# Both query, key and value projections of a four-layer network rebuilt as double-buffered stages, the rotary one in two chunks of eight dimensions

## What is computed

```python
# layer 2
q, k, v = split(layernorm(t) @ W_qkv)            # 16 query heads, 4 key/value heads, 16 wide
# layer 3
g_slc, g_swa = sigmoid(h @ Wg_slc.T), sigmoid(h @ Wg_swa.T)
q, k, v = h @ Wq.T, h @ Wk.T, h @ Wv.T
q = q * cos + rotate_half(q) * sin               # rotate_half([x1, x2]) = [-x2, x1], halves of 8
k = k * cos + rotate_half(k) * sin
out = (softmax(causal(q @ k.T / 4)) @ v) * (g_slc + g_swa)
```

## Time and profile before

| | us |
|---|---|
| median of 3 runs | 2603.23 (2596.47 to 2609.32) |
| the profiled execution, its own time | 2597.99 |
| its span | 2596.3 |
| PE busy / weight loads busy | 2256.7 / 1554.8 |
| DVE / ACT / POOL busy | 1496.3 / 1084.5 / 739.0 |
| layer 2's projection: first matmul to attention's first load | 324.81 to 401.09 |
| layer 3's projection: first matmul to attention's first load | 1387.49 to 1537.88 |

### The profile page before, as it was taken

The page is one execution under the profiler, slowest core; times in us unless marked ns, Lnnn a source line. Parts: engine busy times, 40 slices in busy tenths (PEclk is TensorE's granted clock), DMA queues, the critical chain, the costliest instruction groups (busy, mean ns, idle before and its releaser), DMA issues. The chain is left out here.

```text
span 2596.3 us, 45765 instructions
## 1 busy us (share of the span) xinstructions
PE 2256.7 (87%) x13908; PEld 1554.8 (60%) x13909; DVE 1496.3 (58%) x3329; ACT 1084.5 (42%) x2167; POOL 739.0 (28%) x852
## 2 busy tenths in 40 slices
PE   6979576999977999599957859999865999999997
PEld 5757433444455889599953324444443666666675
DVE  3868747888745766366654658888457222232222
ACT  3434453666634443355532316666530222222222
POOL 1424001222200000388842522222100333333332
PEclk9989797999987999799987869999987999999999
DMA  3000033221102000765651221222046322222211
GB/s 114 1 1 0 7 96 84 54 52 50 39 11 92 1 1 1 186 115 114 97 113 45 61 76 48 54 54 53 9 145 221 82 32 32 33 34 32 34 32 25
DMA packets 134761, 151.40 MB, mean 58 GB/s; under 512 B 32729, under 2 KB 118658, under 8 KB 134274
## 3 DMA queue, kind: packets, MB, share of 16 engines
q1 hardware_dynamic: 105474, 110.19, 14.5%
q0 software_dynamic: 29184, 39.87, 10.0%
HBM read 95.60 MB, written 53.87 MB: 58 GB/s over the span
## 5 line engine op out<-in xcount | busy, mean ns | idle before, releaser
L1250 ACT ACTIVATE L_attn_probs<-L_attn_ps_t 128x512 f32<-128x512 f32 x640 | 374.8, 598 | 245.8 <-PE L_attn_ps_t L1174 240.6
L2368 ACT ACTIVATE L_experts_hiddenT<-L_experts_ps_t,L_experts_b 128x128 f32<-128x128 f32 x576 | 156.3, 382 | 485.4 <-PE L_experts_ps_t L2328 485.4
L1157 PE MATMUL L_attn_ps_m<-L_attn_k,L_attn_q 96*128 96x512 bf16 (+3 forms) x1024 | 282.7, 316 | 52.3 <-DMA L_attn_k<-L_k_parts 45.6
L1120 POOL TENSOR_SCALAR_AFFINE_SELECT L_attn_probs<-L_attn_probs 128x512 f32<-128x512 f32 x256 | 153.2, 634 | 468.2 <-ACT L_attn_probs L1250 468.2
L2337 PE MATMUL L_experts_ps_y<-L_moe_w,L_experts_hiddenT 128*128 x1152 | 260.7, 380 | 2.5 <-ACT L_experts_hiddenT L2368 2.5
L2318 PE MATMUL L_experts_ps_h<-L_moe_w,L_experts_tokenT 128*128 x576 | 260.6, 595 | 0.7 <-issue 0.7
L1157 PEld LDWEIGHTS L_attn_ps_m<-L_attn_k,L_attn_q 96*128 96x128 bf16 x1024 | 101.5, 99 | 259.1 <-issue 89.7
L1174 PE MATMUL L_attn_ps_t<-L_attn_q,L_attn_k 98*128 98x512 bf16 (+3 forms) x1024 | 244.5, 301 | 2.8 <-ACT L_attn_probs L1250 2.3
L2337 PEld LDWEIGHTS L_experts_ps_y<-L_moe_w,L_experts_hiddenT 128*128 128x128 f32 x1152 | 213.5, 190 | 29.1 <-issue 3.3
L2387 DVE COPY L_experts_hidden<-L_experts_ps_h 128x1024 f32<-128x1024 f32 x72 | 88.2, 1225 | 240.6 <-PE L_experts_ps_h L2318 240.6
L1290 DVE TENSOR_REDUCE L_attn_top<-L_attn_ps_m 128x1 f32<-128x512 f32 x256 | 175.4, 685 | 61.7 <-PE L_attn_ps_m L1159 60.5
(11 more groups left out here) (414 smaller groups left out, 5188.7 us busy)
## 6 DMA issues: line engine op xcount, KB each, us to landing
L_q_parts<-L_qkv_parts SPq DMA_DIRECT2D x64, 192.0 KB, 2.7
L_attn_q<-L_q_parts SPq DMA_DIRECT2D x64, 192.0 KB
L_attn_q<-L_q_parts SPq DMA_DIRECT2D x64, 128.0 KB
L_moe_rows<-L_moe_ln_normed SPq DMA_DIRECT2D x16, 512.0 KB, 3.0
L_moe_w<-L_ffn_w SPq DMA_DIRECT2D x2, 4096.0 KB, 18.0
L_moe_w<-L_ffn_w SPq DMA_DIRECT2D x8, 1024.0 KB, 10.7
load_ring<-x SPq DMA_DIRECT2D x8, 512.0 KB, 4.1
L_attn_q<-L_q_parts SPq DMA_DIRECT2D x64, 64.0 KB
```

The source lines that it names most:

```text
L1120: return pool.affine_select(out=block, in_=block, compare_op=ALU.is_ge, fill=0.0, base=0, pattern=columns, channel_multiplier=-1)
L1157: pe.matmul(bank[:, at:at + width], q[j][0:96, head, qb * P:(qb + 1) * P], k[j][0:96, 0:width], start=True, stop=False)
L1250: act.activation(probs[j % 2][:, place[unit], :], ps_t[:, n % 2, :], ACT.Exp, scale=scale).then_inc(exped, 1)
L2368: last = act.activation(hiddenT[:, c, :], ps_t[:, c, :], func, bias=b1[:, ds(e, 1), c])
```

## The change

`project_qkv` is replaced by two functions. In `project_plain` (layer 2) the queries have two buffers in PSUM, the split reads them there, and the keys and the values of two elements are each projected together as two column tiles of 64. In `project_rotary` (layer 3) the weight columns are ordered so that chunk 0 holds the first eight dimensions of every head and chunk 1 the last eight. The rotation of a row is then in the same partition of the other chunk, and the `swap` matmuls, their constant and the copy of the queries fall away. The keys of four elements are projected together as four column tiles of 32 in each chunk. DVE multiplies each item (two chunks of 512) by cosine and sine straight from PSUM, POOL makes one subtraction and one addition of 128x512. All ten items have one shape and go in the order k0, q0 to q3, k1, q4 to q7; each loop is written out. Values and gates of one element share 96 rows. Query stores of layer 3 read 32 partitions with six rows each, where they read 64 with three; keys of four elements are stored in six transfers. What lies in HBM afterwards is the same as before.

```diff
+    width_of = (np.arange(P) % 32 // GR, np.arange(P) % (HD // 2))
     rope = np.stack([f(emb).T[w] for w in width_of for f in (np.cos, np.sin)], 1)
-    swap = np.zeros((P, 2, P), np.float32)
...
-        ahead.swap = ahead.tile("swap", [P, 2, P], dram["c_swap"])
...
-def project_qkv(net, layer, weights, ahead, scratch, values, gates):
+def project_plain(net, weights, ahead, scratch, values):
...
+        ps_q = [net.ps(f"{tag}_ps_q{p}", [P, 2, S], F32, ctx) for p in range(2)]
+        ps_k = net.ps(f"{tag}_ps_k", [P, S], F32, ctx)
+        ps_v = net.ps(f"{tag}_ps_v", [P, S], F32, ctx)
+        ps_turned = net.ps(f"{tag}_ps_turned", [P, TB, P], F32, ctx)
...
+                def project_q(b):
+                    if b >= 2:
+                        pe.wait_ge(q_rested, b - 1)
+                    for c in range(2):
+                        for k in range(KC):
+                            last = pe.matmul(ps_q[b % 2][:, c, :], w[:, k, c * P:(c + 1) * P],
+                                             net.xT[:, k, b * S:(b + 1) * S], start=k == 0, stop=k == KC - 1)
+                    last.then_inc(q_ready, 1)
+                def project_pair(i, out, at):
...
+                        for u in range(2):
+                            b = 2 * i + u
+                            last = pe.matmul(out[64 * u:64 * u + 64, :], w[:, k, at:at + KV],
+                                             net.xT[:, k, b * S:(b + 1) * S], start=k == 0, stop=k == KC - 1,
+                                             tile_position=(0, 64 * u))
...
+                for i in range(PAIRS):
+                    project_q(2 * i)
+                    if i:
+                        turn(i - 1)
+                        pe.wait_ge(k_rested, i)
+                    project_pair(i, ps_k, C).then_inc(k_ready, 1)
+                    project_q(2 * i + 1)
+                    project_pair(i, ps_v, C + KV).then_inc(v_ready, 1)
+                turn(PAIRS - 1)
...
+                for i in range(PAIRS):
+                    high_q(2 * i)
+                    act.wait_ge(k_ready, i + 1)
+                    act.activation(k_parts[i % 2][:, 0, :], ps_k[:, :], ACT.Copy).then_inc(k_high, 1)
+                    middle_q(2 * i)
+                    high_q(2 * i + 1)
+                    act.wait_ge(k_rested, i + 1)
+                    act.activation(k_parts[i % 2][:, 1, :], k_rest[:, :], ACT.Copy).then_inc(k_middle, 1)
+                    act.wait_ge(v_ready, i + 1)
+                    act.activation(v_full[i % 2][:, :], ps_v[:, :], ACT.Copy).then_inc(v_copied, 1)
+                    middle_q(2 * i + 1)
...
+                def rest_q(b):
+                    dve.wait_ge(q_high, b + 1)
+                    if b >= 2:
+                        dve.wait_ge(q_low, b - 1)
+                    dve.tensor_tensor(q_rest[b % 2][:, :, :], ps_q[b % 2][:, :, :], q_parts[b % 2][:, :, 0, :],
+                                      ALU.subtract).then_inc(q_rested, 1)
...
+def project_rotary(net, weights, ahead, scratch, values, gates):
...
+        parts = [sb(f"parts{p}", [P, 3, 2, S], BF16) for p in range(3)]
+        turned_by = [sb(f"turned_by{p}", [P, 2, S]) for p in range(2)]
+        sines = [sb(f"sines{p}", [P, 2, S]) for p in range(2)]
...
+        order = ["k0", 0, 1, 2, 3, "k1", 4, 5, 6, 7]
...
+        DMAS = {n: 6 if isinstance(o, str) else 4 for n, o in enumerate(order)}
...
+            def _(sp):
+                ahead.start(sp)
+                for n, o in enumerate(order):
+                    sp.wait_ge(low, n + 1)
+                    src = parts[n % 3]
+                    if isinstance(o, str):
+                        at = 4 * int(o[1]) * KV
+                        for a in range(3):
+                            to = scratch["k"][a, at:at + 4 * KV, :].rearrange("(v c d) t -> c v d t", c=2, d=HD // 2)
+                            for c in range(2):
+                                sp.dma_start(to[c], src[:, a, c, :]).then_inc(written[n % 3], 16)
+                    else:
+                        for g in range(NKV):
+                            sp.dma_start(scratch["q"][o * NKV + g, :, :].rearrange("(e r) t -> r e t", e=6),
+                                         src[32 * g:32 * g + 32, :, :, :].rearrange("r a c t -> r (a c) t")).then_inc(written[n % 3], 16)
...
+                def project_k(i, n):
+                    if i:
+                        pe.wait_ge(sined, order.index("k0") + 1)
+                    for c in range(2):
+                        for k in range(KC):
+                            for u in range(4):
+                                b = 4 * i + u
+                                last = pe.matmul(ps_k[32 * u:32 * u + 32, c, :],
+                                                 w[:, k, C + HALF * c:C + HALF * (c + 1)],
+                                                 net.xT[:, k, b * S:(b + 1) * S], start=k == 0, stop=k == KC - 1,
+                                                 tile_position=(0, 32 * u))
+                    last.then_inc(k_ready, 1)
+                def project_q(b):
+                    if b >= 2:
+                        pe.wait_ge(sined, order.index(b - 2) + 1)
...
+                def project_vg(b):
+                    if b:
+                        pe.wait_ge(vg_copied, b)
+                    for k in range(KC):
+                        last = pe.matmul(ps_vg[:, :], w[:, k, C + KV:], net.xT[:, k, b * S:(b + 1) * S],
+                                         start=k == 0, stop=k == KC - 1)
+                    last.then_inc(vg_ready, 1)
+                def turn(b):
+                    pe.wait_ge(vg_copied, b + 1)
+                    if b:
+                        pe.wait_ge(values_ready, b)
+                        pe.wait_ge(gate_exp, b)
+                    for t in range(TB):
+                        last = pe.transpose(ps_turned[:, t, 0:VG], vg_full[b % 2][:, t * P:(t + 1) * P],
+                                            net.ident[0:VG, 0:VG])
+                    last.then_inc(vg_turned, 1)
+                for n, o in enumerate(order):
+                    if isinstance(o, str):
+                        project_k(int(o[1]), n)
+                    else:
+                        project_q(o)
+                        project_vg(o)
+                        if o:
+                            turn(o - 1)
+                turn(B - 1)
...
+                for n, o in enumerate(order):
+                    if not isinstance(o, str):
+                        copy_vg(o)
+                    if n:
+                        split_middle(n - 1)
+                    split_high(n)
+                    if not isinstance(o, str) and o:
+                        exp_gates(o - 1)
+                exp_gates(B - 1)
+                split_middle(N_OF - 1)
+            @block.gpsimd
+            def _(pool):
+                for n in range(N_OF):
+                    cosd, sine = turned_by[n % 2], sines[n % 2]
+                    pool.wait_ge(cosines, n + 1)
+                    pool.wait_ge(sined, n + 1)
+                    pool.tensor_tensor(cosd[:, 0, :], cosd[:, 0, :], sine[:, 1, :], ALU.subtract).then_inc(rotated, 1)
+                    pool.tensor_tensor(cosd[:, 1, :], cosd[:, 1, :], sine[:, 0, :], ALU.add).then_inc(rotated, 1)
...
+                for k in range(KC):
+                    for c in range(2):
+                        dve.tensor_copy(
+                            w[:, k, c * P:(c + 1) * P].rearrange("p (g d h) -> p g d h", g=NKV, h=GR),
+                            ps_k[:, k, 0:C].rearrange("p (g h c d) -> p c g d h", g=NKV, h=GR, c=2)[:, c])
+                        dve.tensor_copy(
+                            w[:, k, C + HALF * c:C + HALF * (c + 1)].rearrange("p (g d) -> p g d", g=NKV),
+                            ps_k[:, k, C:C + KV].rearrange("p (g c d) -> p c g d", g=NKV, c=2)[:, c])
+                dve.tensor_copy(w[:, :, C + KV:], ps_k[:, :, C + KV:C + KV + VG]).then_inc(w_ready, 1)
+                def rotate(n):
+                    o = order[n]
+                    at = 2 if isinstance(o, str) else 0
+                    if isinstance(o, str):
+                        dve.wait_ge(k_ready, int(o[1]) + 1)
+                    else:
+                        dve.wait_ge(ready, o + 1)
+                    cosd, bank = turned_by[n % 2], bank_of(n)
+                    if n >= 2:
+                        dve.wait_ge(rested, n - 1)
+                    dve.tensor_tensor(cosd[:, :, :], bank[:, :, :], rope[:, at:at + 1, :].to_broadcast([P, 2, S]),
+                                      ALU.mult).then_inc(cosines, 1)
+                    if n >= 2:
+                        dve.wait_ge(rotated, 2 * n - 2)
+                    dve.tensor_tensor(sines[n % 2][:, :, :], bank[:, :, :],
+                                      rope[:, at + 1:at + 2, :].to_broadcast([P, 2, S]), ALU.mult).then_inc(sined, 1)
+                def take_rest(n):
+                    dve.wait_ge(high, n + 1)
```

(67 more changed lines are left out.)

355 lines of the change are left out of this document (170 added, 185 removed).

## The result

The changed kernel takes 2523.23 us (median of 4 runs, 2519.92 to 2525.17) beside 2599.85 us of the kernel before (4 runs, 2593.66 to 2609.32). The ratio is 0.970, with a 95% interval of 0.967 to 0.974: 3.0% less time. In a second set of runs it took 2520.74 (5 runs) against 2599.55 (9 runs), ratio 0.969 [0.968, 0.971]. The prediction was 2520 us, with a range of 2500 to 2550. The profiled execution took 2524.22 us, with a span of 2522.4.

What follows compares the result with a forecast made beforehand. No engine was full; loops of waits through the engines bound both stages. Saving 19.3 us in layer 2 and 64.1 in layer 3, total 83.4, took 2597.99 to 2514.6; plus 5.2 to the median gave 2520 us, range 2500 to 2550.

Steps and rivals of the forecast that it cites:

- The tail of 2.9: Layer 2: after PE's last work, high, rest, the values' copy, middle and low end 2.9 us later.
- The rule weighed: Layer 2: a tiling mode change drains TensorE; 16 groups paying 0.17 at both borders would add 5 us.
- the 14.8: Layer 3: time until the third item starts, while the pipeline fills, 14.8 us.
- the cold start of 2.8: Layer 3: the first projection runs slow, 8.13 - 5.32 = 2.8 us added to the stretch.
- The 0.4 of weight copies: Layer 3: nine small DVE copies instead of three put the weights in order, adding 0.4 us.
- The two terms: Layer 3, DVE's pace: items with gates 7.45 us each; items without gates 5.8 and 5.9.
- (a): Rival: column tiles run one after another; layer 2 10.6 us longer, layer 3 about 18; 2549 us; chance 0.06.
- (b): Rival, layer 3's DVE-POOL collision: dearer than alternation, 2539 us, chance 0.08; or none, 2512 us, chance 0.05.
- (c): Rival: PE falls to 1.2 GHz for the length of both stages; 2602 us, no change; chance 0.03.
- (d): Rival: 32-partition stores move at a fraction of 246 GB/s, pacing layer 3 beyond 2.3 times, slower kernel at 5.5; chance 0.02.
- the signs named for being wrong: PE waiting for a bank (layer 2), DVE for high (layer 3), tiled group over 1.7, attention over 3 us after last store.
- the term that failed: Attention's loads and everything behind the two changed stretches: untouched, costed at 0.

Runs made afterwards that it cites:

- again: The changed kernel, unaltered, profiled once more beside the kernel before on another day's chip; its profile's span was 2518.9 us.
- sums_under_products: Changed kernel with layer 3's DVE order altered: next item's cosine product and the gates moved between rest and low; 2519.77 us, ratio 0.970.

## Why the prediction held

**Layer 2 (57.0 predicted, 55.4 measured).** PE became the bound, as said. The pair was 11.44, not 11.8: a group of two tiles cost 0.94, not 1.06, and the transposes 0.53, while the query projections, at 3.54 and 3.63, were 0.3 dearer together. The tail of 2.9 was 2.84. The last loads came 380.96 - 378.04 = 2.92 after the last store where 2.56 was taken, but the four stores took 2.57 instead of 3.13 and began 0.03 instead of 0.26 after the low part.

**The rule weighed.** Two untiled query projections (6.88), four tiled groups at one matmul each (4 x 0.86) and the transposes at 0.53 would be 10.85; the pair took 11.44. All borders together thus cost 0.6 a pair, 2.4 us in the stage. The Trainium skill's drain at a change of tiling mode (TensorEngine Tiling (Array Packing), Key Properties) may be what stands behind it, but at half of the 5 us that the estimate made of it.

**Layer 3 (86.3 predicted, 82.9 measured).** DVE became the bound. As it is written, the forecast's list starts with 4.2 for k0 and adds to 81.4; its sum of 77.2 counts the 14.8 from the first matmul, with k0 inside, and so is the measured step. The steps from row to row: 14.4 until the third item (14.8 predicted); 6.8 for the item without gates (5.8); 15.6 for the next two (15.0), with a wait of 1.56 for PE, whose projection at 1396.03 ran at the lower clock; 6.8 for k1 (5.9); 28.0 for four items with gates (29.8); 6.0 for the tail (5.9); 5.3 to attention (5.9). Of the cold start of 2.8 nothing came here (3.64 for k0); where it came (`again`: 6.16, 2.5 more), 1.4 reached the stretch. Without this 2.8 the forecast would have been 83.5; the rest of the difference is small because two terms cancel. The 0.4 of weight copies lies ahead of the first matmul and was counted in the wrong place.

The two terms: items with gates were put at 7.45 and took 6.99. The second sum hides below reciprocal and the gates' sum and delays nothing, and the add of one ends with the first sum where 0.2 was put behind it. Items without gates were put at 5.8 to 5.9 and took 6.8: there nothing separates rest and low. Low waits 1.12 for ACT's middle and then stands behind the second sum (2.32 at 1413.80 where 1.22 is its own). The 5.9 is DVE's work of 4.7 and one of the two sums; the other had been left out together with the gates.

**The collision.** That DVE and POOL exclude each other instruction by instruction was right: the sum's 2.11 is what was left of DVE's rest, 0.99, and then 1.12, near its own 1.26; and the add of one ends at 1420.72, 0.1 after the sum. I had not seen which instructions take part. Products from PSUM, the copy from PSUM and the reciprocal do not; rest, low and the add of one do (and the gates' sum, in `sums_under_products`). The Trainium skill (SBUF — State Buffer, Who interferes with whom) says that a DVE instruction with two SBUF inputs, or a tensor_scalar in a two-port mode, and a GpSimd instruction that reads SBUF keep each other out for a whole instruction. The rows agree: 0.95 instead of 0.22 at the tensor_scalar, and 1.15 for the cosine product at 1415.25 beside POOL's sum, no more than alone.

**The rivals.** (a) Column tiles in sequence: refuted by 0.94 and 3.57. (b) A dearer or a free collision: neither; the sums cost DVE 0.73 once in an item with gates and 1.1 once in an item without. (c) PE at 1.2 GHz: layer 2's clock was 1.00 in the steady part; in layer 3 single projections after a pause ran at the lower level (granted clock 0.58 from 1396 to 1402) and cost one wait of 1.56. (d) Slow stores from 32 partitions: they landed in 3.1 us at the median against 2.7 of the old form, and nothing waited for them. Of the signs named for being wrong two were touched, at no cost to speak of: DVE waited 0.17 for a high part in layer 3, at 1382.12, and attention's first load at 1455.21 came 3.01 us after the end of layer 3's last store issue (1452.20).

**The total.** That the median came out at 2523, 3 us from the forecast, is in part luck. The stretches saved 88.3 in the first pair of profiles and 87.0 on average, where 83.4 was forecast. The time of before was taken as 2603.2, the median of three runs, and averages 2599.9 over 29. Both put the forecast too high, by some 7 us together. Against them stands the term that failed: everything behind the stretches was called untouched and put at nothing, and it took some 9 us back. With the right stretches and the right time before, the same sum would have given 2513.

## What to carry to other kernels

Where no engine is full, look for the loop that runs through all of them within one element; what pays is to move each wait one element away, and the gain, an element, is the period before less the busiest engine's work after, and both can be summed from rows. Do not put the stages that you leave alone at nothing: here they took a tenth of the gain back, and one profile of each kernel could not tell that from chance. With work spread over DVE and GpSimd, sum by kind of operand: products that read PSUM, the copy out of PSUM and the reciprocal did not meet the collision here, so put the helper's work beside those. In-order PE queues deserve a look for one small transpose that waits for another engine: it costs its wait and then the clock of the next projection.

## What the runs showed of the hardware

- Tiled float32 matmuls cost in proportion to their columns in either order: 1.87 us for eight records on tiles of 64, 3.57 for 32 records on tiles of 32, 3.54 to 3.63 for eight untiled ones with tiled groups or transposes behind them, 3.43 with another untiled projection behind them (1381.11 to 1384.54 in layer 3). Without tiles few columns had saved nothing: a record of the old gates' 32 columns took 0.598 (L854 of before), one of 128 columns 0.600.
- DVE's 128x128 add of a constant took 0.22 alone and 0.95 beside GpSimd's sum, its 128x64 sum 0.21 and 1.20; the reciprocal 0.95 either way.
- The same 32 records took from 3.64 to 6.55 us by the clock level met, a program's untouched stages moved by 13 us between profiles of one kernel, and they were some 9 us longer on average once the two stages were changed.
